# Router weights as rows spread by GpSimd instead of a broadcast matmul, in a patch-token, attention and mixture-of-experts kernel

## The reference

```python
pooled = x.reshape(Bb, Cc, n, K, n, K).sum(axis=(3, 5))       # K = 16, n = 14: 196 tokens
h = einsum('bcij,ce->bije', pooled, channel_weights)          # width 192
h = h + attn(layernorm(h))      # q = tokens 0..63, k = v = tokens 64..195; out @ proj_w.T + proj_b
# ffn on layernorm(h): 8 experts of inner width 128 and one shared expert
scores = sigmoid(x2 @ gate_weight.T)                          # groups of 2, top 2 groups, top 2 experts
w = w / (w.sum(-1) + 1e-6);  cw = scatter of w to (token, expert)
y = einsum('tei,edi,te->td', silu(x2 w1) * (x2 w3), w2, cw)
z = silu(x2 @ sw1.T) * (x2 @ sw3.T) @ sw2.T                   # shared expert, no weight
h = h + y + z
```

## Time and profile before

| | us |
|---|---|
| median of 3 runs | 1875.4 (1872.0 to 1878.65) |
| the profiled execution's own time | 1880.6 |
| its span | 1878.9 |
| PE busy | 1634.6 (87%) |
| DVE busy | 1239.9 (66%) |
| ACT busy | 905.8 (48%) |
| POOL busy | 657.5 (35%) |
| mean granted TensorE clock | 0.935 of full |
| DMA traffic | 333.14 MB, 177 GB/s |

### The profile page before, as it was taken

How to read it: one execution, slowest core, us unless ns; L and a number is a source line. 1 busy time by engine, 2 the same in 40 slices (tenths; PEclk the granted TensorE clock), 3 DMA queues, 4 the chain that set the end, 5 groups by cost and what they waited for, 6 DMA issues and landing times.

```text
span 1878.9 us, 31672 instructions
## 1 busy us (share of the span) xinstructions
PE 1634.6 (87%) x9665; PEld 1260.1 (67%) x9798; DVE 1239.9 (66%) x2344; ACT 905.8 (48%) x2999; POOL 657.5 (35%) x739
## 2 busy tenths in 40 slices
PE   1714639999999989998999989998999999999998
PEld 1203528866787667766787667766787678877876
DVE  6855567577666687578566677578666764566365
ACT  2324433656356654656355654656365643443132
POOL 5334326334443435334443335334534332000000
PEclk9955659989999899989999899999999999999999
DMA  8896755546554465555455455556554530000000
GB/s 304 315 352 239 289 219 196 205 165 222 205 204 182 172 222 216 180 200 207 175 205 204 168 215 204 182 198 223 195 205 174 210 131 10 10 18 18 9 19 26
DMA packets 55455, 333.14 MB, mean 177 GB/s; under 512 B 4237, under 2 KB 33666, under 8 KB 33774
## 3 DMA queue, kind: packets, MB, share of 16 engines
q1 hardware_dynamic: 55062, 330.51, 47.6%
q10 hardware_dynamic: 216, 0.50, 0.1%
HBM read 311.10 MB, written 19.27 MB: 176 GB/s over the span
## 4 chain that ended last, share of the span: by engine, by line
PE 69%; DVE 14%; issue 7%; DMA 6%; ACT 2%; POOL 1%; SPq 1%; DVEq 0%; ACTq 0%; another core or an unknown queue 0%; POOLq 0%
PE bank L1370 25%; PE bank L1218 19%; DMA xt<-in_x 6%; PE bank L1392 6%; PE bank L1397 3%; DVE pooled L770 2%; PE bank L1285 2%; DVE ffn L1123 2%; PE bank L1313 2%; DVE ffn L1133 2%; PE bank L1325 2%; PE bank L1274 1%; PE bank L1280 1%; PE bank L1297 1%; PE bank L1290 1%
## 5 line engine op out<-in xcount | busy, mean ns | idle before, releaser
L1370 PE MATMUL bank<-W2T,ffn 128*128 128x192 f32 (+1 forms) x3600 | 692.8, 331 | 0.0
L1370 PEld LDWEIGHTS bank<-W2T,ffn 128*128 128x128 f32 (+1 forms) x3600 | 599.7, 190 | 54.3 <-issue 6.5
L1123 DVE TENSOR_TENSOR ffn<-bank,ffn 128x512 f32<-128x512 f32 (+1 forms) x448 | 278.3, 621 | 367.7 <-PE bank L1218 161.7
L560 POOL TENSOR_TENSOR kh_sum<-xt 128x768 f32<-128x768 f32 (+2 forms) x168 | 249.1, 1483 | 738.0 <-DMA xt<-in_x 730.1
L732 ACT ACTIVATE ffn<-bank 128x512 f32<-128x512 f32 (+1 forms) x504 | 274.1, 547 | 396.0 <-PE bank L1392 211.0
L630 ACT ACTIVATE xt<-xt 128x256 f32<-128x256 f32 x776 | 312.5, 411 | 110.1 <-DMA xt<-in_x 110.1
L1133 DVE TENSOR_TENSOR ffn<-bank,ffn 128x512 f32<-128x512 f32 (+1 forms) x448 | 279.5, 624 | 40.6 <-DVE ffn L1123 33.1
L1392 PE MATMUL bank<-tokT,Wx 126*128 126x512 bf16 (+1 forms) x720 | 250.9, 353 | 25.2 <-DVE ffn L1133 12.6
L770 DVE TENSOR_REDUCE pooled<-xt 128x1 f32<-128x256 f32 (+2 forms) x168 | 233.4, 1389 | 38.9 <-DMA xt<-in_x 38.0
L555 POOL TENSOR_TENSOR kh_sum<-kh_sum 128x384 f32<-128x384 f32 (+2 forms) x336 | 230.2, 685 | 26.4
L1218 PE MATMUL bank<-x0h,WT0h 128*128 128x512 f32 x288 | 154.6, 537 | 3.0 <-issue 2.3
(11 more groups left out here) (253 smaller groups left out, 2161.8 us busy)
## 6 DMA issues: line engine op xcount, KB each, us to landing
xt<-in_x SPq DMA_DIRECT2D x168, 1792.0 KB, 7.3
out<-stage SPq DMA_DIRECT2D x192, 96.0 KB
ffn<-in_L_ffn_w SPq DMA_DIRECT2D x2, 768.0 KB
attw<-in_L_ffn_w SPq DMA_DIRECT2D x1, 512.0 KB
Wx<-tokT ACTq DMA_DIRECT2D x9, 54.2 KB
out<-stage SPq DMA_DIRECT2D x8, 48.0 KB
attw<-in_L_ffn_w SPq DMA_DIRECT2D x1, 256.0 KB
ffn<-in_L_ffn_sw SPq DMA_DIRECT2D x2, 96.0 KB
```

Source lines behind the costliest of these rows:

```text
L560: nc.gpsimd.tensor_tensor(out=kh, in0=src[:, 0:8, :], in1=src[:, 8:16, :], op=ALU.add).then_inc(pool_read, 1)
L1123: v.tensor_tensor(out=gated[p][:, 0:n], in0=h_ps(step, 1)[:, 0:n], in1=silu[p][:, 0:n], op=ALU.mult).then_inc(gated_done, 1)
L1370: last = mm(o, h[step % HR][:, 128 * t:128 * t + m], W2T[:, e, :], start=(e == 0 and query and t % 2 == 0), stop=(e == NE), skip_group_che ...
```

## The change

The weights stay in fp32 and no longer pass PE for each step.

- The gates end after 36 instructions (`GATES`), without the split in bf16. The items C move to steps 57 to 59 and become fp32 transposes of 128x8; ACT copies the results to eight-partition places, and SP stores them to a DRAM tensor `cw_rows`.
- SP loads for each routed step one row of that tensor (1 partition, 512 or 64 values) into a ring of 7 buffers, five steps ahead, in its one queue, behind the tile load of the same step.
- POOL spreads the row over the 128 partitions in place (`partition_broadcast`) a step ahead, and multiplies silu by it when silu is ready (`scale`). DVE has one product a step, `h = h3 * scaled silu`, for the shared expert with silu itself.
- The broadcast matmul, `sel`, `cwT`, `cw_ps`, `gated` are gone. The bank that comes free makes h1 and h3 go round four banks; PE no longer waits for silu before h3, and starts h1 of step s when the product of step s-2 is done.
- From the third group on (and the last two tiles of the second) POOL has no part in the pooling. DVE has 9 blocks, as 5 in the tile's step and 4 in the next, and ACT has 5, as 3 and 2.
- POOL's two large powers of a group (98x32) are cut into halves, one a step from step 4 to 7.

```diff
-SHARE = {"dve": (0, 7), "act": (7, 9), "pool": (9, NP)}
-SHARE_K = {"dve": (0, 1), "act": (1, 8), "pool": (8, NP)}
+SHARE = {"dve": [(0, 5), (5, 9)], "act": [(9, 12), (12, NP)], "pool": None}
-    59: [("C", 0), ("C", 1)],
-    60: [("C", 2), ("C", 6)],
-    61: [("C", 3), ("C", 4), ("C", 5)],
+    57: [("C", 0), ("C", 1)],
+    58: [("C", 2), ("C", 6)],
+    59: [("C", 3), ("C", 4), ("C", 5)],
-GATES = 40
+GATES = 36
+CW_RING = 7
+CW_AHEAD = 5
...
+                    slot_free(use + 1 if use + 1 in (NE, CW_USES) else use)
+                at = col if query else 1024 + col
+                sp.dma_start(cwb[slot][0:1, 0:n], cw_rows[g.par, e:e + 1, at:at + n]).then_inc(cw_landed[slot], 16)
...
                     for gt_, t in tiles_at(g, step, left):
                         load_after(gt_, t)
+                    cw_ahead(g, step, left)
...
+                pool.wait_ge(spread, g.at(CW_USES, use + 1))
+                pool.wait_ge(silu_done, g.at(STEPS, step + 1))
+                nc.gpsimd.tensor_tensor(out=cwb[slot][:, 0:n], in0=silu[(g.par + step) % 2][:, 0:n],
+                                        in1=cwb[slot][:, 0:n], op=ALU.mult).then_inc(scaled, 1)
...
+                pool.wait_ge(cw_landed[slot], g.at(16 * CW_USES // CW_RING, 16 * (use // CW_RING + 1)))
+                pool.sem_inc(pool_passed, 1)
+                nc.gpsimd.partition_broadcast(cwb[slot][:, 0:n], cwb[slot][0:1, 0:n]).then_inc(spread, 1)
...
                 for step in range(STEPS):
+                    scale(g, step)
+                    if step + 1 < STEPS:
+                        spread_row(g, step + 1)
+                    elif left:
+                        spread_row(g.plus(1), 0)
                     step_pool(g, step, left)
...
-                        v.tensor_tensor(out=gated[p][:, 0:n], in0=h_ps(step, 1)[:, 0:n], in1=silu[p][:, 0:n],
-                                        op=ALU.mult).then_inc(gated_done, 1)
...
-                        v.tensor_tensor(out=h[step % HR][:, 0:n], in0=cw_ps[:, 0:n], in1=gated[p][:, 0:n],
-                                        op=ALU.mult).then_inc(h_done, 1)
+                    v.tensor_tensor(out=h[step % HR][:, 0:n], in0=h_ps(g, step, 1)[:, 0:n],
+                                    in1=(silu[p] if e == NE else cwb[(c * NE + e) % CW_RING])[:, 0:n],
+                                    op=ALU.mult).then_inc(h_done, 1)
...
-                    if e < NE:
-                        wait(pe, h_done, g.at(NCH * NE, c * NE + e))
-                        at = col if query else 1024 + col
-                        mm(cw_ps[:, 0:n], sel[:, e, :], cwT[:, at:at + n], start=True, stop=True).then_inc(cw_ready, 1)
```

More of the change, by code:

```diff
@@ L148, in share, with pool_sums @@
 def share(g, t):
[L150 to L153, removed]
+    return SHARE0 if pool_sums(g, t) else SHARE
+def pool_sums(g, t):
+    return g.k is None and g.off * TILES + t < POOL_TILES
 def tiles_at(g, step, groups_left=2):
@@ L475, in load_after, with cw_rows_out, cw_load, slot_free @@
                     load(g.plus(1), t + SLOTS - TILES)
+            def cw_rows_out(g, step):
+                for kind, i in items_at(step):
+                    if kind == "C":
+                        n = 512 if i < 6 else 64
+                        sp.wait_ge(aux_act, g.at(BYACT[-1], BYACT[R[("C", i)]]))
+                        sp.dma_start(cw_rows[g.par, :, 512 * i:512 * i + n], cw_stage[i][:, 0:n])\
+                          .then_inc(cw_out[1 if i else 0], 16)
+            def cw_load(g, step):
+                c, e = divmod(step, EX)
+                if e == NE:
+                    return
+                query, col, n = CHUNKS[c]
+                use = c * NE + e
+                slot = use % CW_RING
+                def slot_free(use):
+                    back = use - CW_RING
+                    wait(sp, h_done, g.at(STEPS, back // NE * EX + back % NE + 1))
+                if use == 0:
+                    sp.wait_ge(cw_out[0], g.at(16, 16))
+                elif use == NE:
+                    sp.wait_ge(cw_out[1], g.at(96, 96))
+                else:
+                    slot_free(use + 1 if use + 1 in (NE, CW_USES) else use)
+                at = col if query else 1024 + col
+                sp.dma_start(cwb[slot][0:1, 0:n], cw_rows[g.par, e:e + 1, at:at + n]).then_inc(cw_landed[slot], 16)
+            def cw_ahead(g, step, left):
+                if left:
+                    cw_rows_out(g.plus(1), step)
+                if step + CW_AHEAD < STEPS:
+                    if g.off >= 0:
+                        cw_load(g, step + CW_AHEAD)
+                elif left:
+                    cw_load(g.plus(1), step + CW_AHEAD - STEPS)
             def ffn_dma(g, left):
@@ L490, in _ @@
                     load_after(gt_, t)
+                cw_ahead(G(None, -1), step, 1)
             ffn_dma(G(None, 0), 2)
@@ L604, in _ @@
             ffn_pool(G(None, 6), 1)
+            ffn_pool(G(None, 7), 0)
         @block.scalar
@@ L712, in step_act @@
             def step_act(g, step, left):
[L714 to L720, removed]
+                for back in (1, 0):
+                    for gt_, t in tiles_at(g, step - back, left):
+                        parts = share(gt_, t)["act"]
+                        if back < len(parts):
+                            act_tile(gt_, t, *parts[back], back == len(parts) - 1)
                 if left:
@@ L729, in ffn_act @@
                     act.wait_ge(h1_ready, g.at(STEPS, step + 1))
-                    wait(act, gated_done, g.at(STEPS, step - 1))
+                    wait(act, h_done, g.at(STEPS, step - 1))
                     p = (g.par + step) % 2
-                    nc.scalar.activation(silu[p][:, 0:n], h_ps(step, 0)[:, 0:n], ACT.Silu).then_inc(silu_done, 1)
+                    nc.scalar.activation(silu[p][:, 0:n], h_ps(g, step, 0)[:, 0:n], ACT.Silu).then_inc(silu_done, 1)
                     if e == 1 and c > 2:
```

184 lines of the change are left out of this document (97 added, 87 removed).

## The result

| | before | after |
|---|---|---|
| median, us | 1877.0 (1872.0 to 1881.3) | 7254.6 (7250.4 to 7262.6) |
| ratio | 1 | 3.866 (95%: 3.858 to 3.875) |
| span of the profiled execution | 1878.9 | 7250.4 |
| PE busy | 1634.6 (87%) | 2412.9 (33%) |
| DVE busy | 1239.9 (66%) | 1067.2 (15%) |

The account below looks back on a forecast made before the run. PE was taken to bound the middle and end, DVE the gate stretch. Terms -63 + 39 + 5 + 5 = -14 us against 1880.6 gave 1866, or 1861 for the median; own range 1840 to 1885, whole range 1805 to 1945.

Parts of the forecast that it names:

- POOL's step ... 2.08 us: POOL's routed step: multiply 1.28 us, broadcast 0.7 and two hops of 0.05, over PE's 1.74 and the old 1.95.
- anything further up: Chance 0.04 for outcomes slower than the forecast and named rivals; the whole range ended at 1945 us.
- the term of steps 36 to 44: Key steps where PE is full: dropping broadcast matmuls saves 12 us, 8 x 7 x 0.21.
- 0.21 us per broadcast matmul: PE time freed per removed full broadcast matmul, from key steps of 1.95 us with one and 1.74 without.
- nothing and costs nothing: Last group's four key chunks: POOL's pace of 16.6 us a chunk against 17.3 before, counted as 0.
- The halved powers ... I count 0 of it, at most 1 us a group: Four query steps: POOL's 2.7 us half powers make it 4.6 us late, mostly absorbed; counted 0, at most 1 us a group.
- the stretch grows by about 6.5 us: DVE in the gate stretch, steps 45 to 56: bounds 0 and 16 us; +39 us over six groups with tiles.
- forecast +5: Seventh gate stretch, without tiles: POOL's 21 us and 24 locked gates don't overlap, 30 us in all, +5.
- the lock: Gate stretch: two-SBUF-input DVE gates wait for a running POOL instruction, 7.5 us a group against some 3.9 before, +3.6.
- Rows on SP's queue: Row loads queue behind tile loads in key steps; counted 0, bound 0 to 2 us for each of six tiles.
- rival 2: Rows come late: 1 us for each of six tiles in six groups, 36 us, giving 1897 us; chance 0.18.
- Head, +5: Kernel start: gates and set-up removed, about -2; first weights' two trips through DRAM, +7; sum +5 us.

Follow-up runs that it names:

- e_row_mix: Changed kernel with one POOL library loaded once; first three rows of a group loaded by SP ahead of the tile, others by ACT; 1901.5 us (1.0122).
- e_dma_mix: Changed kernel, but DMA spreads rows to 128 partitions, without POOL's broadcast; first three rows of a group from SP, others from ACT; 1886.1 us (1.0043).
- b_pooling: Kernel before with only the pooling shares changed: POOL out, DVE 5 + 4 blocks, ACT 3 + 2; 1902.9 us (1.0127).
- e_rows_actq: As e_onelib, but ACT issues the row loads through its own queue at the end of its step; 1931.7 us (1.030).
- e_onelib: Changed kernel plus one load, ahead of POOL's loops, of the library holding both multiply and broadcast; 1968.9 us (1.048).
- m_switch: POOL's multiply and broadcast with nothing else on the chip, alternating or one kind in a row; alternating gaps 7.2 us before multiplies, 6.0 before broadcasts.

## Why the prediction was wrong

**The step that failed: "POOL's step ... 2.08 us".** It is the sum of a multiply, a broadcast and two hops, and it counts nothing between the instructions. With the changed kernel's libraries a step of POOL is 15.5 us in the timeline. No row of before could show this: POOL's rows there are adds, powers, selects and casts, and none of them has such gaps before it. The chances did not hold it either: "anything further up" had 0.04. The Trainium skill had it: "GPSIMD Engine Reference", section "Instruction dispatch", says that the first call to a freshly loaded kernel pays an IRAM load of about 6 us (5.95 measured there), with no visible profile instruction. The traces here agree, with 6.0 us before a broadcast and a little more, 7.2, before a multiply. What the Trainium skill does not say is which instructions share a library; with that doubt alone the rule belonged among the rivals. As an estimate from the Trainium skill's 6 us, its price would have been 896 x 6 = 5376 us.

**The other steps, on the mended change.** Since e_row_mix has only the faults taken out, its parts can be held against the forecast's. The marks are the starts of the first and the last recorded matmul with the query weights (L1218 before, L1327 in e_row_mix, L1323 in e_dma_mix), 180 of them in each group's query steps, and of the first of the ten gate-logit matmuls on the same line in the middle of the key steps, which part these in two. The forecast's terms are laid on the same stretches: the first row has the head's +5 with one group's terms, the term of steps 36 to 44 is halved between the two rows of key steps, and rounding is left as it falls. Microseconds of the profiled executions:

| stretch | before | b_pooling | e_dma_mix | e_row_mix | forecast | e_row_mix less before |
|---|---|---|---|---|---|---|
| start to the second group | 485.3 | 490.0 | 490.4 | 494.1 | +3 | +8.8 |
| six groups, query steps | 490.0 | 485.3 | 484.8 | 486.5 | -20 | -3.5 |
| six groups, to the ten matmuls | 401.0 | 409.4 | 393.8 | 404.4 | -15 | +3.5 |
| six groups, from there (gates) | 344.0 | 363.9 | 366.5 | 358.3 | +22 | +14.3 |
| last group | 158.6 | 158.5 | 151.3 | 154.9 | -3.4 | -3.6 |
| span | 1878.9 | 1907.2 | 1886.8 | 1898.3 | -14 | +19.4 |

- **0.21 us per broadcast matmul: right.** In the last group silu starts are 3.64 us apart in query steps, 3.87 before.

```profile
1793.12 0.60 ACT L855 ACTIVATE ffn<-bank 128x512 f32<-128x512 f32 x1 [3.04 <-PE bank L1327]
1796.76 0.60 ACT L855 ACTIVATE ffn<-bank 128x512 f32<-128x512 f32 x1 [3.04 <-PE bank L1327]
...
1845.43 0.60 ACT L855 ACTIVATE ffn<-bank 128x512 f32<-128x512 f32 x1 [1.53 <-PE bank L1498]
1847.55 0.60 ACT L855 ACTIVATE ffn<-bank 128x512 f32<-128x512 f32 x1 [1.52 <-PE bank L1498]
```

- **A POOL step of 2.08 us, once the library is right: right, and its cost was too.** The last two rows are key steps: 2.12 us, POOL's pace, where PE alone does 1.74 (e_dma_mix). From the first silu of the last group's key steps to the end it is 91.5 us in e_row_mix and 91.5 before (the 17.3 us of the prediction for a chunk of before leaves out its slower first steps), so "nothing and costs nothing" came out. In the middle groups it did not: up to the ten matmuls e_row_mix is 10.6 us over e_dma_mix, which was not counted; 8.3 of it comes back behind them, where PE waits less for the last gate. Those 10.6 us and the 8.4 that the pooling shares cost there by themselves (b_pooling) are what stands between the -15 forecast and +3.5.
- **"The halved powers ... I count 0 of it, at most 1 us a group": wrong, some 3 us.** The first 17 query steps of the second group (start to start) sum to 77.2 us in b_pooling and 77.3 in e_row_mix. Fifteen of them are 3.0 us shorter, as the 0.21 says, and the eighth and ninth 3.1 longer (4.34 to 6.71 and 4.78 to 5.49). The timeline of e_row_mix in the eighth:

```profile
519.50 3.01 POOL L628 TENSOR_TENSOR stat<-stat,mhalf 98x16 f32<-98x16 f32 x1
522.37 1.39 POOL L653 TENSOR_TENSOR ffn<-ffn 128x512 f32<-128x512 f32 x1
```

```profile
523.96 0.69 DVE L1241 TENSOR_TENSOR ffn<-bank,ffn 128x512 f32<-128x512 f32 x1 [3.09 <-POOL ffn L653]
524.56 0.18 DVE L1034 TENSOR_TENSOR stat<-stat,keymask 98x32 f32<-98x32 f32 x1
...
525.55 0.56 DVE L1040 TENSOR_TENSOR PH<-Ptok,stat 98x384 f32<-98x384 f32 x1
```

```profile
526.16 0.56 PE L1373 MATMUL bank<-ident,PH 98*128 98x98 f32 x4 [2.47 <-DVE PH L1040]
```

  The half power stands before the multiply on POOL, DVE waits 3.09 us for the multiply with the statistics queued behind its product, and PE waits 2.47 for the statistics' result. The working looked for the reader of h, two steps away; the first to be late was what stood behind the product on DVE. In the six groups the two steps are 20 us longer than in b_pooling, and 15 longer than in the kernel before, whose eighth step was itself slower (5.1 to 5.5 us in five of the six). That is most of the 20 that the query steps were to give. Most of it is there without a broadcast too (5.9 and 5.5 us in e_dma_mix). This is read from the timelines; no run puts the powers elsewhere.
- **DVE in the gate stretch, "the stretch grows by about 6.5 us": wrong, 0.6 us.** From the start of the first gate to the end of the 36th, the six stretches that have tiles beside them take 31.3 us on average before and 31.9 in e_row_mix; the one without tiles takes 24.7 and 26.1 (forecast +5). Two terms were too large. The sum of DVE's parts is +5.6, and 0.9 us of idle was put on top of it, though that stood already in the 29 us. And the lock, forecast to cost 3.6 us more a group, costs none more: the 36 gates themselves take 16.7 us before, 16.4 in e_row_mix, and 12.2 in b_pooling, where POOL is idle beside them. What the 31.9 us still hide is the pooling: b_pooling takes 33.7. The question that the prediction left open, whether a broadcast locks too, is answered by a gate (L1167) that meets a broadcast only, and by its like (L1171) a little later:

```profile
672.58 0.79 POOL L666 PARTITION_BROADCAST ffn<-ffn  x1
...
672.66 0.79 DVE L1167 TENSOR_TENSOR gt<-gt,gs 128x200 f32<-128x200 f32 x1
...
673.88 0.37 DVE L1171 TENSOR_TENSOR gt<-gt,gs 128x200 f32<-128x200 f32 x1
```

  The first ends 0.08 us after the broadcast and takes 0.79 us instead of 0.37; it does so in four of the eight groups. So a broadcast locks too.
- **The pooling's cost elsewhere: left out.** b_pooling loses 8.4 us in the six groups up to the ten matmuls, where I had put nothing, and 8.5 behind the 36th gate. Presumably 5 and 4 blocks on DVE are longer than the 1 block and the finish also where no gates run; ACT's share changed in the same run, and the two are not told apart.
- **Rows on SP's queue, "I count 0": wrong.** 37 us by e_rows_actq against e_onelib, beside the 36 of rival 2, which had 0.18; 67 us by e_row_mix, in which ACT's wait at the turn of a group is gone too. It is the largest part of the 92 us that e_onelib is over before.
- **The transposes, not priced.** PE waits for the last gate in each group, 2.8 us in e_row_mix and 4.5 in e_dma_mix, where the kernel before has no such wait outside the head; the transposes now stand two steps earlier. In fp32 they take 313 ns each, and the bf16 ones before 231.
- **Head, +5: about right.** The first query matmul starts at 277.6 us before and at 284.2 in e_row_mix; it is 278.9 in e_dma_mix, so the two trips through DRAM can't be most of it. To the second group it is +8.8, of which the pooling shares alone are 4.7.

In short: the forecast was off by 5400 us. With the library fault alone taken out (e_onelib) it would have been 108 us off, and outside its range; with the late rows out as well (e_row_mix) 40 us, in its range but on the wrong side of the kernel before. That it lies so near even then is partly luck: the gate stretch was some 6 us a group too dear, and the powers, the broadcasts up to the ten matmuls and the pooling outside the gates were put at nothing. No version that was run beats the kernel before; the nearest is e_dma_mix at +0.4%.

## What to carry to other kernels

Before an instruction of another kind joins a programmable engine's loop, ask whether both kinds live in the same code library, look in the built program's instruction list for loads, and multiply their price by the number of changes; the profile of the old kernel did not show it, since nothing changed libraries there. Where a profile's idle time is put down to "issue" on one engine and stands before each instruction of that engine at a change of kind, this is the first suspect, and one explicit load of a library with both is the test. And when a producer moves to a queue with large transfers in it, its latency is theirs: two kilobytes took 7.9 us here behind a tile.

## What the runs showed of the hardware

- A change of library on POOL costs 7.2 us before a multiply and 6.0 before a broadcast (m_switch); the single explicit load showed a gap of 5.2.
- A broadcast of one row of 512 fp32 values over 128 partitions takes POOL 0.80 us, one multiply of 128x512 fp32 1.25 us alone and 1.28 in the full kernel.
- A DVE instruction with two SBUF inputs waits for POOL's broadcast as it does for POOL's adds: 0.79 us instead of 0.37 (e_row_mix).
- A broadcasting DMA of 262 KB in 384 steps brings the DMA rate to 260 GB/s in a middle group, from 198 before. The tiles then land in 8.1 us (median) instead of e_row_mix's 7.2, and e_dma_mix is still the fastest variant.
